# One decoder layer in a software pipeline on one core: the written-out order of four engines is replaced by another

## The chip, the cores and the metric

The kernel runs on 1 core of one Trainium2 chip. The time is device microseconds (us) of that core, from the start to the end of one launch. Five engines work side by side, each taking its own instructions strictly in program order: TensorE (PE in the profile; its weight loads stand apart as PEld), VectorE (DVE), ScalarE (ACT), GpSimd (POOL) and SyncE (SP, which here only starts DMAs). They wait for one another on semaphores alone.

## The reference

The input x is 64 sequences of 128 rows of 512 numbers, in f32. Three blocks, each with a residual and a layer norm in front of it:

```python
x = x + _L0_attn_ref(_layernorm(x), ...)            # state-space mixer
x = x + _L0_xattn_ref(_layernorm(x), ctx, ..., 64)  # banded attention, gated by ctx
x = x + _L0_ffn_ref(_layernorm(x), ...)             # 8 experts, the best 2 used
```

The mixer, with I = 1024 channels, N = 16 states per channel and R = 128:

```python
proj = x @ in_proj_w.T ; h_in, gate = split(proj)
u  = silu(causal_conv4(h_in) + conv_b)
ts, Bm, Cm = split(u @ x_proj_w.T)
dt = softplus(ts @ dt_proj_w.T + dt_proj_b)
dA = exp(dt[..., None] * -exp(A_log)) ; dBx = (dt * u)[..., None] * Bm
h  = scan(h * dA + dBx)                   # along the 128 rows
y  = ((h * Cm).sum(states) + D * u) * silu(gate)
out = y @ out_proj_w.T
```

The attention has 8 heads of 16 over a band of 64 to either side, then relu, a product with ctx and one more matrix. The last block is a softmax router over 8 experts with 16 hidden channels each.

## The kernel before

**Groups.** The 64 sequences are taken two at a time: 32 groups (`NG`). Within one iteration of every engine's program up to four groups are in work: the scans of group g (`cur`), the projections and step sizes of group g+1 (`nxt`), the attention of group g-1 (`p1`) and the experts of group g-2 (`p2`). Iterations -1, 0, 1 and the last four are written out, the others stand in a hardware loop of two iterations each.

**The core of it: 64 scan steps per group.** Step s is one block of 128 channels (`ic = s // 8`) and one pair of states (`r = s % 8`), 512 numbers per partition. For each step
- ACT writes the decays into one of two PSUM slots (`decays`, two `Exp` of L474, the slot is `s % DAR`). It may do so when scan s-2 is done; where the state of s-2 was kept in PSUM (`s % 8` in 1, 4, 7), when DVE's product with C is done too (L470 then clears the first column);
- POOL writes dt·u·B into one of eight ring slots in SBUF (`times_b`, L306), once PE has added up step s-8 (`hc_used`);
- DVE runs the scan (`scan`, L1498);
- the product with C is POOL's (`times_c`, L315, 40 steps) or DVE's (`times_c`, L1482, 24 steps, those with `s % 8` in 1, 4, 7);
- PE adds the products of two steps at a time by transposing matmuls into PSUM (`y_sum`, L1114).

**The other work** stands between these steps: `h_in`, `gate_in`, `ts_in`, `dt_in`, `out_proj` and the parts of the attention (`proj`, `v`, `s`, `shift`, `st`, `av`, `den`, `rep`, `wo`, `ct`) on PE; conv (L1601), the maxima of the scores (`max`, L1520), `addq`, `on`, `enc`, `x2`, the router and `y_step` (L1491) on DVE; the exps of the attention (L628), silu (L580 of u, L593 of the gate, L645 of the experts), copies out of PSUM and norms on ACT.

**The step size.** softplus is taken apart: ACT makes |z|, exp, +1 and ln (`soft_exp`, `soft_one`, `soft_ln`), DVE four steps per pair of channel blocks (`soft_step` 1 to 4: L1466, L1469, L1473, L1477), 128x512 each. These sixteen DVE instructions per group read two tensors that both lie in SBUF; the scans, L1482 and the conv read one of their operands from PSUM. `soft_step(4)` makes du, for which `times_b` waits at every 16th step.

**ScalarE's tables.** Exp, Silu and Ln need a table each; the compiler puts an ACT_TABLE_LOAD ahead of the first function of another kind. A stretch of another table between two `decays` is called an excursion here: one load to get there, one to come back.

**What sets the order.** Nothing at run time: `iteration(g, cur, nxt, p1, p2)` of each engine is a list of calls written out by hand, with the work of the four groups interleaved. SP's list is not touched.

Of the kernel before, what the change touches and what calls it, by code (L numbers as in the profile page):

```python
# [5 lines left out]
def decoder_layer(nc, x_d, ctx_d, w_in_d, conv_w_d, conv_b_d, w_xt_d, w_xbc_d, w_dt_d, dt_b_d, a_log_d,  # L6
# [40 lines left out]
    with stack:  # L47
# [233 lines left out]
        def _(pool):  # L281
# [37 lines left out]
            def iteration(g, cur, nxt, p1, p2):  # L319
                if p1:  # L320
                    times_c(g - 1, 62)
# [3 lines left out]
                if p2:  # L325
                    rstd("e", g - 2, 0, 2)
                if cur:
                    times_b(g, 2)
                    times_b(g, 3)
                    times_c(g, 0)  # L330
# [6 lines left out]
                    times_b(g, 8)  # L337
                    times_b(g, 9)
                    times_b(g, 10)
                    times_c(g, 5)  # L340
                if p1:
                    rstd("t", g - 1, 0)
                if cur:
                    times_b(g, 11)
                    times_b(g, 12)
                    times_b(g, 13)
                    times_c(g, 6)
                    times_c(g, 8)
                    times_c(g, 10)
                    times_b(g, 14)  # L350
                    times_c(g, 11)
                    times_b(g, 15)
                if nxt:
                    rstd("a", g + 1, 0, 2)
                if cur:
                    times_b(g, 16)
                    times_b(g, 17)
                    times_c(g, 13)
                    times_b(g, 18)
                    times_c(g, 14)  # L360
                    times_b(g, 19)
                    times_b(g, 20)
                    times_c(g, 16)
                    times_c(g, 18)
                    times_b(g, 21)
                    times_b(g, 22)
                    times_b(g, 23)
                    times_b(g, 24)
                    times_c(g, 19)
# [3 lines left out]
                    times_b(g, 26)  # L373
                if p1:
                    rstd("t", g - 1, 1)
                if cur:
                    times_b(g, 27)
# [3 lines left out]
                    times_b(g, 30)  # L381
                    times_c(g, 26)
                    times_c(g, 27)
                    times_b(g, 31)
                    times_c(g, 29)
                    times_b(g, 32)
                    times_c(g, 30)
                    times_b(g, 33)
                    times_b(g, 34)
                    times_b(g, 35)  # L390
                    times_c(g, 32)
                    times_b(g, 36)
                    times_b(g, 37)
                    times_b(g, 38)
                    times_c(g, 34)
                    times_b(g, 39)
# [7 lines left out]
                    times_b(g, 44)  # L404
# [1509 lines left out]
```

How the kernel before makes its waits and increments, by code:

```python
        def reached(engine, semaphore, count):  # L194
            if not (isinstance(count, int) and count <= 0):
                engine.wait_ge(semaphore, count)
# [25 lines left out]
            def iteration(g, cur, nxt, p1, p2):  # L223
# [5 lines left out]
                    piece(1, 0)  # L229
                if p1:
                    context((g - 1) * GB)
                if cur:
                    for r in range(NSPREAD, RS):
                        spread(g, r)
                if nxt:
                    reached(sp, gin_ps, j * NQ)
                    piece(0, 1)
                if p2:
                    sp.wait_ge(x3_done, (g - 1) * GB)
                    sp.dma_start(rows(out_d, g - 2), x_att[:]).then_inc(x_out, 16)
                if nxt:
                    sp.wait_ge(hin_ps, j * NQ + 1)
                    piece(1, 2)
                    sp.wait_ge(hin_ps, j * NQ + 2)
                    piece(0, 3)
                    sp.wait_ge(gin_ps, j * NQ + 1)
                    piece(1, 4)
                    sp.wait_ge(hin_ps, j * NQ + 3)
                    piece(0, 5)
                if p1:
                    context((g - 1) * GB + 1)
                if nxt:
                    sp.wait_ge(gin_ps, j * NQ + 2)
                    piece(1, 6)
                    sp.wait_ge(hin_ps, j * NQ + 4)
                    piece(0, 7)
                    sp.wait_ge(bc_made, j + 1)
                    for c in range(4):
                        sp.dma_start(bc_d.rearrange("r (k t) -> (r k) t", k=4)[:, c * (NT // 4):(c + 1) * (NT // 4)],
```

## Time and profile before

| | us |
|---|---|
| median of 3 runs (lowest, highest) | 5135.03 (5134.79, 5142.79) |
| the profiled execution, its own time | 5140.37 |
| its span in the profile | 5138.5 |
| granted TensorE clock over the span | 0.975 of full speed |
| busy: PE / DVE / POOL / ACT | 4659.6 / 4631.4 / 4395.1 / 4216.9 |

Four engines are busy for 82% to 91% of the span, so no one of them is plainly the bound. The start (until the first scan at 104 us) and the end (after the last one, near 4983 us) are thinly filled; between them the same pattern repeats, once per group. A period of the pattern is best read off a DMA that SP starts once per group, the store of the result.

### The profile page before, as it was taken

To read this page: it belongs to the slowest core of one execution; us is meant where nothing else is said; L and a number is where in the kernel's file an instruction comes from. 1 tells how busy PE (TensorE), PEld (TensorE's weight loads), DVE (VectorE), ACT (ScalarE), POOL (GpSimd) and SP (SyncE) were. 2 spreads that over 40 slices of the span, in tenths; PEclk is the share of its full clock that TensorE was granted. 3 is DMA by queue.
4 is the path that set the end of the run, shared out by engine and by line. 5 is a ranking of instruction groups with operands and counts; after the bars stand their busy time and mean duration, and the time that the engine had idled before them with its cause. 6 is when DMAs were issued, how large, how long until landed. Compare 5 with 4: busy or idle time off the path is not lost.

```text
span 5138.5 us, 143326 instructions
## 1 busy us (share of the span) xinstructions
PE 4659.6 (91%) x52548; PEld 3356.2 (65%) x52548; DVE 4631.4 (90%) x6051; ACT 4216.9 (82%) x8962; POOL 4395.1 (86%) x3467
## 2 busy tenths in 40 slices
PE   4799999999999999999999999999999999999986
PEld 3566666666666766666666666666666666666653
DVE  3899999999999999999999999999999999999962
ACT  3788888888888888888888888888888888888862
POOL 2988998988898988999988998898889898889870
PEclk8899999999999999999999999999999999999986
DMA  3212222212222211222221222221222221222200
GB/s 120 77 41 71 69 76 79 80 47 69 74 75 76 80 62 54 75 73 76 79 80 37 79 69 80 79 80 40 77 69 75 80 80 49 67 73 72 67 10 11
DMA packets 119316, 350.46 MB, mean 68 GB/s; under 512 B 18688, under 2 KB 19456, under 8 KB 118528
## 3 DMA queue, kind: packets, MB, share of 16 engines
q1 hardware_dynamic: 118656, 341.51, 20.2%
q8 instruction: 432, 7.08, 0.6%
q14 instruction: 228, 1.87, 0.1%
HBM read 323.64 MB, written 17.83 MB: 66 GB/s over the span
## 4 chain that ended last, share of the span: by engine, by line
PE 44%; issue 16%; POOL 16%; DVE 12%; ACT 11%; POOLq 0%; DVEq 0%; ACTq 0%; DMA 0%
POOL ring L306 10%; PE ps L1162 8%; PE ps L1114 6%; POOL ring L315 5%; PE ps L1182 5%; PE ps L1058 4%; PE ps L1069 3%; PE ps L1030 3%; DVE nmax L1520 3%; DVE ring L1498 3%; ACT ps L474 2%; PE ps L1005 2%; ACT probs_mem L628 2%; DVE hc L1601 2%; PE ps L1094 2%
## 5 line engine op out<-in xcount | busy, mean ns | idle before, releaser
L306 POOL TENSOR_TENSOR ring<-du,bc 128x512 f32<-128x512 f32 x2048 | 2640.6, 1309 | 374.6 <-PE ps L1114 276.8
L315 POOL TENSOR_TENSOR ring<-ring,bc 128x512 f32<-128x512 f32 x1280 | 1715.4, 1350 | 185.6 <-DVE ring L1498 180.2
L474 ACT ACTIVATE ps<-delta,a_neg 128x254 f32<-128x254 f32 x4096 | 1767.6, 469 | 114.7 <-DVE ring L1498 103.5
L1498 DVE TENSOR_TENSOR_SCAN ring<-ps,ring 128x512 f32<-128x512 f32 x1280 | 1536.2, 1211 | 45.6 <-ACT ps L474 30.8
L1114 PE MATMUL ps<-ident,ring 128*128 128x128 f32 x8192 | 1090.0, 279 | 45.1 <-POOL ring L315 39.7
L1114 PEld LDWEIGHTS ps<-ident,ring 128*128 128x128 f32 x8192 | 932.4, 143 | 243.8 <-issue 172.3
L1498 DVE TENSOR_TENSOR_SCAN ps<-ps,ring 128x512 f32<-128x512 f32 x768 | 935.2, 1218 | 123.6 <-ACT ps L474 119.0
L1482 DVE TENSOR_TENSOR ring<-ps,bc 128x512 f32<-128x512 f32 x768 | 526.4, 685 | 12.4
L1182 PE MATMUL ps<-w_in,xt_a 128*128 128x256 f32 x2048 | 484.6, 391 | 37.7 <-ACT yz L562 20.1
L628 ACT ACTIVATE probs_mem<-ps 128x768 f32<-128x768 f32 (+1 forms) x512 | 441.8, 908 | 52.6 <-PE ps L1058 50.1
L1162 PE MATMUL ps<-xt_a,w_in 128*128 128x256 f32 x2048 | 476.8, 386 | 7.4 <-DVE hc L1601 4.1
L1144 PE MATMUL ps<-w_outp,yz 128*128 128x512 f32 x1024 | 467.1, 599 | 6.7 <-DVE x_att L1544 6.7
L1182 PEld LDWEIGHTS ps<-w_in,xt_a 128*128 128x128 f32 x2048 | 387.0, 194 | 114.2 <-issue 43.9
L1520 DVE TENSOR_REDUCE nmax<-ps 128x8 f32<-128x1280 f32 x256 | 379.8, 1484 | 68.5 <-PE ps L1030 61.8
L1162 PEld LDWEIGHTS ps<-xt_a,w_in 128*128 128x128 f32 x2048 | 382.1, 191 | 80.8 <-issue 25.4
L1601 DVE SCALAR_TENSOR_TENSOR hc<-ps,conv_w,hc 128x254 f32<-128x254 f32 (+2 forms) x768 | 360.5, 473 | 63.2 <-ACT hc L573 42.2
L470 ACT COPY ps<-zeros 128x4 f32<-128x4 f32 x768 | 126.9, 165 | 251.0 <-DVE ring L1482 244.4
L1144 PEld LDWEIGHTS ps<-w_outp,yz 128*128 128x128 f32 x1024 | 189.2, 192 | 205.6 <-issue 193.9
L1030 PE MATMUL ps<-qk 32*32 32x160 f32 (+2 forms) x16384 | 294.6, 296 | 0.0
L1058 PE MATMUL ps<-qk 32*128 32x192 f32 (+1 forms) x4096 | 274.4, 383 | 0.0
L1005 PE MATMUL ps<-xb,w_qk 128*128 128x512 f32 x512 | 252.8, 607 | 15.4 <-ACT qk L615 12.6
L1069 PE MATMUL ps<-probs_mem,v_aug 128*32 128x192 f32 (+1 forms) x4096 | 229.0, 366 | 10.2 <-ACT probs_mem L628 10.2
(139 smaller groups left out, 6550.3 us busy)
## 6 DMA issues: line engine op xcount, KB each, us to landing
w_in<-in_w_in SPq DMA_DIRECT2D x256, 512.0 KB, 3.6
bc<-bc_rows SPq DMA_DIRECT2D x256, 512.0 KB, 5.9
x_new<-in_x SPq DMA_DIRECT2D x32, 512.0 KB, 6.1
x_res<-in_x SPq DMA_DIRECT2D x32, 512.0 KB, 5.0
enc<-in_ctx SPq DMA_DIRECT2D x64, 256.0 KB, 3.8
out<-x_att SPq DMA_DIRECT2D x32, 512.0 KB, 3.0
w_outp<-in_w_outp SPq DMA_DIRECT2D x1, 2048.0 KB, 8.2
bc_rows<-bc_sb SPq DMA_DIRECT2D x128, 8.0 KB, 1.4
```

What stands on the lines that cost most here:

```text
L306: nc.gpsimd.tensor_tensor(ring[:, s % RING, :].rearrange("p (n t) -> p n t", n=2), du[:, q % 2, (ic % 2) * NT:(ic % 2 + 1) * NT].rearrange ...
L315: nc.gpsimd.tensor_tensor(ring[:, s % RING, :], ring[:, s % RING, :], bc[:, s % RS, 2:4, :].rearrange("p a t -> p (a t)"), ALU.mult).then_ ...
L474: nc.scalar.activation(ps[:, s % DAR, (n % 2) * NT:(n % 2 + 1) * NT].rearrange("p (b t) -> p b t", b=GB)[:, :, 1:T], delta[:, ic, :].rearr ...
L628: nc.scalar.activation(probs[:, :, blk, lo:hi], ps[:, PS_ATT:PS_ATT + 4, (n % 2) * WIN + lo:(n % 2) * WIN + hi], ACT.Exp).then_inc(p_done, 1)
L1058: last = nc.tensor.matmul(ps[:, PS_ATT + hp, a * WIN + lo:a * WIN + hi], qk[r:r + 32, 2 + j, blk * P:(blk + 1) * P], qk[r:r + 32, j, at:at ...
L1114: last = nc.tensor.matmul(ps[:, PS_Y, b * T:(b + 1) * T], ring[:, t % RING, n * NT + b * T:n * NT + (b + 1) * T], ident[:], start=False, s ...
L1144: last = nc.tensor.matmul(ps[:, PS_ATT + b, :], yz[:, ic, b * T:(b + 1) * T], w_outp[:, ic, :], start=(ic == 0), stop=(ic == NI - 1))
L1162: last = nc.tensor.matmul(ps[:, PS_B, a * NT:(a + 1) * NT], w_in[:, slot, k, a * P:(a + 1) * P], xt_a[:, k, :], start=(k == 0), stop=(k == ...
L1182: last = nc.tensor.matmul(ps[:, PS_B, b * NT:(b + 1) * NT], xt_a[:, k, b * T:(b + 1) * T], w_in[:, slot, k, :], start=(k == 0), stop=(k == ...
L1482: nc.vector.tensor_tensor(ring[:, s % RING, :], ps[:, s % DAR, :], bc[:, s % RS, 2:4, :].rearrange("p a t -> p (a t)"), ALU.mult).then_inc ...
L1498: nc.vector.tensor_tensor_scan(state, ps[:, s % DAR, :], ring[:, s % RING, :], 0.0, ALU.mult, ALU.add).then_inc(h_done, 1)
L1520: nc.vector.tensor_reduce(nmax[:, n].rearrange("p j (a r) -> p a j r", r=32)[:, :, :, DH], ps[:, PS_ATT:PS_ATT + 4, 0:NJ * NEAR].rearrange ...
```

## The change

In `iteration` of POOL, ACT, PE and DVE the calls stand in another order. Every call is there as often as before, with the same arguments, so the same buffers and the same semaphores; SP's list and all helper functions are as they were. ScalarE's helper functions stand one line higher up than before, PE's four lines further down, DVE's where they were. As the order decides where ScalarE changes its table, the number of table loads is not the same: 60 in the program before, 72 now, which is 10 and 12 in one iteration with all four groups.

The diff is 1185 lines of moved calls; its shape, in DVE's list:

```diff
                 if cur:
                     scan(g, 4)
                     times_c(g, 4)
+                    soft_step(1, g, 2)
+                    scan(g, 5)
                     soft_step(4, g, 1)
-                    scan(g, 5)
                     scan(g, 6)
+                    soft_step(2, g, 2)
                     scan(g, 7)
...
                 if cur:
-                    scan(g, 60)
+                    times_c(g, 60)
+                if p1:
+                    attention(g, 1, "x2")
                 if nxt:
                     soft_step(1, j, 0)
```

and in PE's, second sequence of the attention:

```diff
                 if p1:
                     attention(g, p2, 1, "s", 3)
-                if cur:
-                    y_sum(g, 35)
-                    y_sum(g, 37)
+                if nxt:
+                    h_in(j, 3, cur)
                 if p1:
                     attention(g, p2, 1, "shift")
```

**VectorE, the end of iteration 1.** `L1498` is a scan, `L1482` DVE's product with C, `L1538` is `enc`, `L1544` is `x2` of the second sequence, `L1466`, `L1469`, `L1473` and `L1477` are `soft_step` 1 to 4 of group g+1. Before:

```order
L1538 SCALAR_TENSOR_TENSOR o_sb<-ps,enc 128x512
L1498 SCALAR_TENSOR_TENSOR ps<-ps,ring 128x512
L1466 SCALAR_TENSOR_TENSOR tmp<-tmp,soft 128x512
L1482 TENSOR_TENSOR ring<-ps,bc 128x512
L1466 SCALAR_TENSOR_TENSOR tmp<-tmp,soft 128x512
L1498 SCALAR_TENSOR_TENSOR ring<-ps,ring 128x512
L1469 SCALAR_TENSOR_TENSOR delta<-delta,tmp 128x512
L1498 SCALAR_TENSOR_TENSOR ring<-ps,ring 128x512
L1473 TENSOR_TENSOR delta<-delta,soft 128x512
L1544 SCALAR_TENSOR_TENSOR x_att,ln_sum_e<-ps,b_ct,x_res 128x512
L1477 TENSOR_TENSOR du<-delta,u 128x512
L1498 SCALAR_TENSOR_TENSOR ps<-ps,ring 128x512
```

The same place now, to the end of the iteration:

```order
L1538 SCALAR_TENSOR_TENSOR o_sb<-ps,enc 128x512
L1482 TENSOR_TENSOR ring<-ps,bc 128x512
L1544 SCALAR_TENSOR_TENSOR x_att,ln_sum_e<-ps,b_ct,x_res 128x512
L1466 SCALAR_TENSOR_TENSOR tmp<-tmp,soft 128x512 x2
L1469 SCALAR_TENSOR_TENSOR delta<-delta,tmp 128x512
L1498 SCALAR_TENSOR_TENSOR ring<-ps,ring 128x512
L1469 SCALAR_TENSOR_TENSOR delta<-delta,tmp 128x512
L1498 SCALAR_TENSOR_TENSOR ps<-ps,ring 128x512
L1473 TENSOR_TENSOR delta<-delta,soft 128x512
L1477 TENSOR_TENSOR du<-delta,u 128x512
L1482 TENSOR_TENSOR ring<-ps,bc 128x512
L1473 TENSOR_TENSOR delta<-delta,soft 128x512
```

The soft steps stood one by one between scans; three now follow each other ahead of scan 62, and two with the last product and one more behind scan 63, while `x2` comes two instructions after `enc`.

**ScalarE, the last silu of u in iteration 1.** `L573` is conv's first tap, `L580` silu of u, `L593` silu of the gate, `L562` and `L632` are copies out of PSUM, `L474` decays, `L628` exps of the attention. Before:

```order
L573 ACTIVATE hc<-ps,conv_b,conv_w 128x256 x2
L632 COPY o_sb<-ps 128x512
L580 ACT_TABLE_LOAD
L580 ACTIVATE u<-hc 128x512
L593 ACTIVATE gate_t<-gate_t 128x2x512
L580 ACTIVATE u<-hc 128x512
L562 COPY yz<-ps 128x256
L470 COPY ps<-zeros 128x4
L474 ACT_TABLE_LOAD
L474 ACTIVATE ps<-delta,a_neg 128x2x127 x4
```

Now (the same functions are one line number lower):

```order
L473 ACTIVATE ps<-delta,a_neg 128x2x127 x2
L627 ACTIVATE probs_mem<-ps 128x4x256
L627 ACTIVATE probs_mem<-ps 128x4x192
L473 ACTIVATE ps<-delta,a_neg 128x2x127 x2
L579 ACT_TABLE_LOAD
L579 ACTIVATE u<-hc 128x512
L561 COPY yz<-ps 128x256
L631 COPY o_sb<-ps 128x512
L469 COPY ps<-zeros 128x4
L473 ACT_TABLE_LOAD
L473 ACTIVATE ps<-delta,a_neg 128x2x127 x4
```

One excursion with three silus has become a short one with one silu, two decays later; the silu of the gate has an excursion of its own five decays earlier, and the third silu went to the others of u.

## Rows read from the trace of the kernel before

**Rows 1.** The page: its head, and each engine's busy us (share) xinstructions.
```profile
span 5138.5 us, 143326 instructions
PE 4659.6 (91%) x52548; PEld 3356.2 (65%) x52548; DVE 4631.4 (90%) x6051; ACT 4216.9 (82%) x8962; POOL 4395.1 (86%) x3467
```

**Rows 2.** Busy time by stretch: PE, PEld, DVE, ACT, POOL, clock, DMA share, GB/s.
```profile
2420.40:3031.40 611.00, 572.38 (x6568) 413.55 (x6568) 578.51 (x757) 526.35 (x1120) 549.76 (x433) 1.00 0.22 71
```

**Rows 3.** Timeline of SP: start, duration, issue of the result's store, four groups apart.
```profile
2420.42 0.40 SPq L240 DMA_DIRECT2D out<-x_att  x1
...
3031.38 0.40 SPq L240 DMA_DIRECT2D out<-x_att  x1
```

**Rows 4.** Groups of DVE, 2420.4 to 3031.4: busy us, mean ns, idle before.
```profile
L1498 DVE TENSOR_TENSOR_SCAN ring<-ps,ring 128x512 f32<-128x512 f32 x160 | 192.1, 1211 | 3.1 <-ACT ps L474 2.0 <-POOL ring L306 0.9
...
L1482 DVE TENSOR_TENSOR ring<-ps,bc 128x512 f32<-128x512 f32 x97 | 66.5, 685 | 1.5
...
L1601 DVE SCALAR_TENSOR_TENSOR hc<-ps,conv_w,hc 128x254 f32<-128x254 f32 (+2 forms) x96 | 45.1, 473 | 2.6
L1466 DVE SCALAR_TENSOR_TENSOR tmp<-tmp,soft 128x512 f32<-128x512 f32 x16 | 19.4, 1212 | 0.0
L1469 DVE SCALAR_TENSOR_TENSOR delta<-delta,tmp 128x512 f32<-128x512 f32 x16 | 17.5, 1091 | 0.0
L1473 DVE TENSOR_TENSOR delta<-delta,soft 128x512 f32<-128x512 f32 x16 | 17.2, 1074 | 0.0
L1477 DVE TENSOR_TENSOR du<-delta,u 128x512 f32<-128x512 f32 x16 | 13.5, 842 | 0.0
L1491 DVE TENSOR_TENSOR yg<-ps,gate_t 128x256 f32<-128x256 f32 x32 | 13.1, 408 | 0.0
```

**Rows 5.** One line's instructions, same stretch: duration ns min/median/max.
```profile
L1473 DVE TENSOR_TENSOR delta<-delta,soft x16: 659/914/1815, 2438.7 to 2996.1; 128x512 f32<-128x512 f32 x16
```

**Rows 6.** Timeline, one soft step of DVE and POOL's neighbours.
```profile
2531.40 1.28 POOL L306 TENSOR_TENSOR ring<-du,bc 128x512 f32<-128x512 f32 x1
2531.41 1.81 DVE L1473 TENSOR_TENSOR delta<-delta,soft 128x512 f32<-128x512 f32 x1
...
2532.62 1.73 POOL L315 TENSOR_TENSOR ring<-ring,bc 128x512 f32<-128x512 f32 x1
```

**Rows 7.** Timeline, the end of ScalarE's longest excursion; brackets: idle before, releaser.
```profile
2504.20 1.28 ACT L474 ACT_TABLE_LOAD   x1
...
2505.49 1.66 ACT L474 ACTIVATE ps<-delta,a_neg 128x254 f32<-128x254 f32 x4
2506.39 1.23 DVE L1498 TENSOR_TENSOR_SCAN ps<-ps,ring 128x512 f32<-128x512 f32 x1 [2.93 <-ACT ps L474]
```

**Rows 8.** Groups of ACT, 2420.4 to 3031.4.
```profile
L562 ACT COPY yz<-ps 128x256 f32<-128x256 f32 x32 | 11.8, 369 | 15.6 <-PE ps L1135 15.6
...
L580 ACT ACTIVATE u<-hc 128x512 f32<-128x512 f32 x16 | 10.0, 626 | 0.1
...
L632 ACT COPY o_sb<-ps 128x512 f32<-128x512 f32 x16 | 9.3, 583 | 4.4 <-PE ps L1069 4.4
```

**Rows 9.** Timeline of DVE: two waits for PE, at `max` and at `experts_add`.
```profile
2479.76 1.49 DVE L1520 TENSOR_REDUCE nmax<-ps 128x8 f32<-128x1280 f32 x1 [1.16 <-PE ps L1030]
...
2572.65 0.69 DVE L1508 TENSOR_TENSOR x_att<-ps,x_att 128x512 f32<-128x512 f32 x1 [1.35 <-PE ps L1235]
```

**Rows 10.** Timeline of PE: one `h_in`, and its wait for the router.
```profile
2469.65 3.72 PE L1182 MATMUL ps<-w_in,xt_a 128*128 128x256 f32 x16
...
2568.55 0.65 PE L960 MATMUL ps<-ident,probs_mem 128*128 128x128 f32 x2 [1.55 <-DVE probs_mem L1590]
```

**Rows 11.** Timeline of the start: POOL's first product with B, the first scan.
```profile
98.09 5.77 POOL L306 TENSOR_TENSOR ring<-du,bc 128x512 f32<-128x512 f32 x4 [74.23 <-DVE du L1477]
...
104.17 1.22 DVE L1498 TENSOR_TENSOR_SCAN ring<-ps,ring 128x512 f32<-128x512 f32 x1 [3.88 <-ACT ps L474]
```

More of the change, by code:

```diff
@@ L827, in iteration @@
                 if cur:
-                    decays(g, 42)
-                if p1:
-                    attention(g, p2, 1, "exp", 0)
-                    attention(g, p2, 1, "exp", 1)
-                if cur:
-                    decays(g, 43)
                     decays(g, 44)
@@ L838, in iteration @@
                     decays(g, 45)
+                if nxt:
+                    gate_silu(j, 0)
+                if cur:
+                    decays(g, 46)
+                    decays(g, 47)
+                if nxt:
+                    tap3(j, 3)
+                if cur:
+                    skip_term(g, 7)
+                if p1:
+                    attention(g, p2, 1, "exp", 0)
+                    attention(g, p2, 1, "exp", 1)
+                if cur:
+                    decays(g, 48)
+                    decays(g, 49)
                 if p1:
@@ L856, in iteration @@
                     y_back(g, 4)
-                    decays(g, 49)
-                    decays(g, 50)
+                if p1:
+                    attention(g, p2, 1, "o", 0)
+                if cur:
+                    decays(g, 51)
+                    decays(g, 52)
                 if p1:
@@ L1265, in iteration @@
                     attention(g, p2, 0, "proj", 0)
+                    attention(g, p2, 0, "proj", 1)
+                if cur:
+                    y_sum(g, 5)
+                if p2:
+                    experts_gate(g - 2)
+                if p1:
+                    attention(g, p2, 0, "v")
+                if p2:
+                    experts_up(g - 2)
                 if cur:
@@ L1346, in iteration @@
                 if p1:
-                    attention(g, p2, 1, "s", 1)
+                    attention(g, p2, 0, "wo")
+                    attention(g, p2, 1, "proj", 1)
+                if cur:
+                    y_sum(g, 31)
                 if nxt:
@@ L1370, in iteration @@
                 if cur:
[L1371 to L1373 removed]
+                    y_sum(g, 47)
+                    y_turn(g, 4, nxt)
                 if p1:
@@ L1675, in iteration @@
                     scan(g, 18)
-                if p1:
-                    attention(g, 0, "max", 2)
-                if cur:
-                    scan(g, 19)
                     y_step(g, 1)
@@ L1697, in iteration @@
                 if cur:
+                    scan(g, 23)
+                if nxt:
+                    conv(j, 1)
+                if cur:
+                    times_c(g, 23)
                     scan(g, 24)
@@ L1734, in iteration @@
                 if cur:
-                    scan(g, 34)
+                    scan(g, 37)
+                    y_step(g, 3)
+                    scan(g, 38)
+                    scan(g, 39)
                 if p1:
@@ L1779, in iteration @@
                     conv(j, 6)
+                if cur:
+                    scan(g, 48)
+                if nxt:
                     conv(j, 7)
                 if cur:
-                    scan(g, 48)
+                    y_step(g, 5)
                     scan(g, 49)
@@ L1793, in iteration @@
                     times_c(g, 55)
+                    scan(g, 56)
+                    scan(g, 57)
+                    y_step(g, 6)
+                    times_c(g, 57)
                 if p1:
@@ L1802, in iteration @@
                 if cur:
-                    y_step(g, 6)
-                    scan(g, 58)
-                    scan(g, 59)
+                    scan(g, 60)
+                    scan(g, 61)
                 if p1:
```

551 lines of the change are left out of this document (255 added, 296 removed).

## The prediction, made before the changed kernel ran

> **What bounds the kernel now.** The page's first part comes first: PE, DVE and POOL are busy for 86% to 91% of the span [rows 1]. That is a mean over a thin start, 32 groups and a thin end, so the next view is the timeline of SP: the store of the result is issued at 2420.42 and, four groups later, at 3031.38 [rows 3]. A group takes 610.96 / 4 = 152.74 us. The busy time over the same stretch [rows 2] divided by four gives, per group, PE 143.1, DVE 144.6, POOL 137.4, ACT 131.6; idle are PE 9.6, DVE 8.1, POOL 15.3, ACT 21.2. So DVE has the least air, PE nearly as little, and a new order can gain in two ways alone: fewer of DVE's 8.1 idle microseconds, or DVE instructions that themselves take less. 32 groups have 31 distances between them; with 31 I multiply.
>
> The second way exists. DVE's groups [rows 4] show the scan at 1211 ns, and the four soft steps, which read two operands from SBUF, at 1212, 1091, 1074 and 842 ns. The shortest of L1473 took 659 ns, the longest 1815 [rows 5]. The timeline shows why [rows 6]: this longest one is entered at 2531.41, just after a POOL product that started at 2531.40 and took its usual 1.28; it ends at 2533.22, that is 0.54 us after the POOL product, and the next POOL product, entered at 2532.62, takes 1.73 in place of 1.28. The two take turns. The scans show nothing of it, they are as long beside POOL as without.
>
> **The change, part by part, in us per group.**
>
> (a) *Soft steps.* The mean of the four is (1212 + 1091 + 1074 + 842) / 4 = 1055 ns; alone it would be 659. Each pays 0.40, all sixteen 6.3. To be rid of it a soft step has to stand where POOL waits. Now three of group g+1 follow one another between `x2` and scan 62. POOL has at most one product with C (of step 61) and one with B (63) left then, since the next, step 62's, waits for scan 62. The first soft step meets a product, the second and third should not. Behind scan 63 POOL's next product with B is step 0 of the next group and waits for du, so `soft_step` 3 and 4 ahead of that should be free too. One more, `soft_step(4, g, 3)`, follows `addq` of the second sequence, where POOL waits for the `y_sum` behind PE's long block. Five of sixteen, 5 x 0.40 = -2.0. The bounds are 0 (POOL late at all of them) and -6.3 (all sixteen free). I take -2.0, since the other eleven stand between scans as before.
>
> (b) *ScalarE's longest excursion.* At scan 49 DVE waits 2.93 for decays that come behind two silus of u, one of the gate and a reload [rows 7]. Now the silu of the gate has an excursion of its own, with a scan, a maximum and a product of DVE beside it, and the last silu of u stands between decays 50 and 51. From the end of scan 48, ACT does decays 50 (a pair, 1.66 / 2 = 0.83 [rows 7]), load 1.28, silu 0.63, two copies 0.37 and 0.58 [rows 8], load 1.28, decays 51 0.83: 5.8. DVE has in the meantime three conv taps (3 x 0.47), `y_step` 0.41, two scans of 1.21, one product 0.69 [rows 4]: 4.9 by durations, some 4.5 as they overlap at their ends. It waits about 1.4. Gain 2.93 - 1.4: -1.5. Bounds: -2.9 and 0.
>
> (c) *Table loads.* Two more per group, 2 x 1.28 = 2.6 on ACT [rows 7]. The decays are issued at most two scans ahead, so an excursion costs when DVE has less than its length to do; the three new borders lie beside conv, maxima and `addq`. Cost 0, covered by ACT's 21.2 idle; 2.6 if that cover were gone. In the timeline the first exp follows the load's start by 1.29 us (2504.20 to 2505.49 [rows 7]), so 1.28 is the whole price. The Trainium skill, "ScalarE: Activation LUTs", section "What ACT_TABLE_LOAD costs", says about 1283 ns of load plus 1380 ns of drain, 2.66 us for every switch; the load agrees to the nanosecond, the drain is not there in this trace. By the page the excursion of (b) would last 2.8 longer and eat its gain of 1.5, and the sum below would come out near +0.8 in place of -2.0; the trace decides.
>
> (d) *DVE's waits for PE that go.* 1.16 at the third `max` of the second sequence and 1.35 at `experts_add` [rows 9]. The first came from an `h_in` that PE did ahead of those scores; now they follow the `max` before with two sums between, while DVE has two scans and a product. The second came from a `y_sum` ahead of `experts_up`, which now stands behind it. -2.5, bounds 0 and -2.5.
>
> (e) *New short waits.* Five places where DVE now asks sooner for what another engine has just been told to do: `router(1)` directly behind `router(0)` (an exp of ACT lies between); `x2` two instructions after `enc` (PE's `ct` lies between); `soft_step(3)` of g+1, whose `soft_ln` moved behind a gate copy to the very end of ACT's list; `addq` of both sequences, as `h_in` was put ahead of `shift` on PE. The trace has no such waits; the nearest rows are 1.16 and 1.35 [rows 9], the largest 2.93 [rows 7], the least is 0. I take 0.8 each, below the nearest rows since part is covered by the instructions between: +4.0; bounds 0 and 5 x 2.93 = 14.7.
>
> (f) *PE and POOL.* PE gets 9.6 idle and its list has the same work. In its early part `out_proj` of the second sequence and the norm's transposes went ahead of `y_sum(1)`, so the sums of steps 1 to 7 come about 5 us later, and POOL waits for these before step 9 to 15. Their cover is that DVE has the router before scan 11 now. PE's own wait for the router, 1.55, stays. Cost 0; if the cover is gone, up to one `h_in`, 3.72 [rows 10].
>
> Sum: -2.0 - 1.5 - 2.5 + 4.0 = -2.0 per group, 31 x -2.0 = -62.
>
> (g) *Start and end.* POOL begins at 98.09, the first scan at 104.17 waits 3.88 for ACT [rows 11]. Now du comes about 2 us later (ACT does the third step size and the gate copy before `soft_ln`), but the decays follow it after one step size instead of a copy, a skip term and a step size. First scan some 2 us earlier: -2. The end has the same chain of attention and experts: 0, within 5 either way.
>
> The profiled execution's own time is 5140.4, 5.3 above the median. 5140.4 - 64 = 5076; against the median of 5135.0 that is 5071. I say 5073.
>
> **The rivals.**
>
> *R1, slower: a whole `h_in` between `s` and `shift`.* In both sequences PE has `h_in` (3.72 [rows 10]) between the last scores and the transposes for which `addq` waits. DVE used to have one scan (first sequence) or one conv (second) between its fourth `max` and `addq`, now two scans and one scan. If DVE is as early as before, it waits 3.72 less one scan of 1.21 in the first and all 3.7 in the second, 6.2 together. With the other three waits of (e) at 0.8 that makes -2.0 - 1.5 - 2.5 + 2.4 + 6.2 = +2.6 per group, +81, less 2: 5219 of its own, 5214 against the median. It decides from 3.6 on (the two waits together), where the sum is 0. For it: DVE is the fullest engine and cannot catch up. Against it: PE lags DVE by several scans, `h_in` could start while the fourth `max` runs, and the wait that leads to the sum is also taken off elsewhere (`st` no longer has `h_in` behind it).
>
> *R2, even: given back.* The waits of (e) come to 1.2 each (the nearest rows' size): 6.0, the sum is 0.0. Or POOL is late and (a) gives nothing. 5135. For it: in the stretch all four engines are busy for 86% or more [rows 2], so what one gains another soon asks for.
>
> *R3, the waits of (e) are all covered.* -2.0 - 1.5 - 2.5 = -6.0, x 31 = -186, less 2: 4952 of its own, 4947. For it: DVE would be idle 2 us of some 147, which no stretch of this trace comes near to. Half way, 5010, is more likely.
>
> *R4, the ports are not what the order serves.* POOL gets late by other waits and the soft steps stay at 1055 ns; (b) and (d) still hold: the sum is 0, as R2, which includes it.
>
> **How the numbers follow.** Forecast 0.45, with a range of its own from 5020 to 5120. R3 and half of it 0.14 (4947 to 5020). R2 with R4 0.14 (5120 to 5150). R1 0.27 (5146 to 5215 and above). What a measurement of this kernel can tell from no change is 0.2%, 10 us. Faster: 0.45 + 0.14 + 0.03 of R2 = 0.62; same: 0.09; slower: 0.27 + 0.02 = 0.29. The range leaves out some 0.07 below and 0.12 above: 4985 to 5190.
>
> **What would show it.** The store of the result every 150.7 us in place of 152.7. (a) L1466 to L1477 at a mean near 930 ns in place of 1055, and of the six soft steps of g+1 up to du, four near 0.66. (b) No DVE wait for ACT of over 2 us; one near 1.4 at scan 51. (c) 12 table loads per group, the exp right behind each. (d) the third `max` and `experts_add` without a wait. (e) waits of 0.5 to 1.4 at `addq`, `x2`, `soft_step(3)` and the router; R1 is right if the two `addq` wait 3.6 or more together, R3 if none waits. (f) POOL's waits for `y_sum` in the early part stay under 2. The forecast is wrong in its base if DVE's idle time per group grows above 11 us.

## The result, and the profile after

| | before | after |
|---|---|---|
| median (lowest, highest) of 4 runs each | 5136.00 (5134.79, 5142.79) | 5098.34 (5097.39, 5103.19) |
| the profiled execution, its own time | 5140.37 | 5097.39 |
| ratio, 95% interval | | 0.9926, [0.9909, 0.9943] |

The changed kernel is 38 us faster, against 62 forecast. The page's head after, to be held against [rows 1]:

```profile
span 5095.5 us, 143390 instructions
PE 4632.5 (91%) x52548; PEld 3377.4 (66%) x52548; DVE 4539.5 (89%) x6051; ACT 4303.2 (84%) x9026; POOL 4273.2 (84%) x3467
```

DVE has the same 6051 instructions and is busy 92 us less; ACT has 64 instructions more, the table loads. A stretch of four groups, from store to store (timeline of SP) and its busy times, answers to [rows 2, 3]:

```profile
2402.13 0.40 SPq L240 DMA_DIRECT2D out<-x_att  x1
...
3009.50 0.40 SPq L240 DMA_DIRECT2D out<-x_att  x1
```

```profile
2402.10:3009.50 607.40, 570.70 (x6568) 417.01 (x6568) 565.89 (x757) 537.04 (x1129) 534.12 (x433) 0.99 0.22 71
```

A group takes 607.37 / 4 = 151.84 in place of 152.74. DVE is busy 141.5 of it (before 144.6) and idle 10.4 (before 8.1): its instructions became 3.1 shorter, and 2.3 of that went into waits. Only 0.9 of the 3.1 is in the soft steps (67.6 us before and 63.8 now in four groups). Most of the rest is in three small instructions of the router, of which the prediction had nothing: before, they ended with a product of POOL (L1574 of 2564.85 ended at 2565.73, 0.03 behind one), and now POOL mostly waits beside them. They took 10.6 us in four groups and take 3.6, 1.8 less per group. Two of them, before:

```profile
L1581 DVE COPY small<-small 128x4 f32<-128x4 f32 x4 | 3.4, 851 | 0.1
L1574 DVE TENSOR_TENSOR small<-small 128x16 f32<-128x16 f32 x4 | 3.0, 756 | 0.6 <-DVE small L1572 0.6
```

and after:

```profile
L1581 DVE COPY small<-small 128x4 f32<-128x4 f32 x4 | 0.7, 170 | 0.1
L1574 DVE TENSOR_TENSOR small<-small 128x16 f32<-128x16 f32 x4 | 0.9, 232 | 0.1
```

The third is L1590, from 558 to 287 ns, eight times. The groups of DVE in this stretch, to be held against [rows 4]:

```profile
L1498 DVE TENSOR_TENSOR_SCAN ring<-ps,ring 128x512 f32<-128x512 f32 x160 | 192.3, 1210 | 16.8 <-ACT ps L473 15.8
...
L1473 DVE TENSOR_TENSOR delta<-delta,soft 128x512 f32<-128x512 f32 x16 | 30.0, 1877 | 4.5 <-ACT soft L547 4.5
...
L1469 DVE SCALAR_TENSOR_TENSOR delta<-delta,tmp 128x512 f32<-128x512 f32 x16 | 11.7, 734 | 0.0
L1466 DVE SCALAR_TENSOR_TENSOR tmp<-tmp,soft 128x512 f32<-128x512 f32 x16 | 11.3, 725 | 0.0
L1477 DVE TENSOR_TENSOR du<-delta,u 128x512 f32<-128x512 f32 x16 | 10.8, 674 | 0.1
```

Three of the four soft steps now take little more than the 0.66 us of one that meets no product of POOL (725, 734 and 674 ns). The fourth kind, L1473, went from 1074 to 1877. The view of that one line says that it is not all of them:

```profile
L1473 DVE TENSOR_TENSOR delta<-delta,soft x16: 672/1119/4600, 2433.3 to 2978.5; 128x512 f32<-128x512 f32 x16
```

One of the four per group takes 4.6 us. It is `soft_step(3, g, 2)`, behind scan 27. The timeline around it, DVE and POOL:

```profile
2432.38 1.28 POOL L306 TENSOR_TENSOR ring<-du,bc 128x512 f32<-128x512 f32 x1
2433.31 4.59 DVE L1473 TENSOR_TENSOR delta<-delta,soft 128x512 f32<-128x512 f32 x1
2433.61 2.51 POOL L315 TENSOR_TENSOR ring<-ring,bc 128x512 f32<-128x512 f32 x2
...
2436.07 1.28 POOL L306 TENSOR_TENSOR ring<-du,bc 128x512 f32<-128x512 f32 x1
...
2437.82 1.22 DVE L1498 TENSOR_TENSOR_SCAN ps<-ps,ring 128x512 f32<-128x512 f32 x1
...
2440.83 1.26 POOL L315 TENSOR_TENSOR ring<-ring,bc 128x512 f32<-128x512 f32 x1 [3.48 <-DVE ring L1498]
```

The step is entered while a product runs, POOL starts three more back to back, none of them longer than alone (2.51 for two), and the step ends at 2437.90, 0.55 behind the end of POOL's last at 2437.35. It had no turn in between. Then POOL waits 3.48 for the scans behind the step: POOL had held up the engine that it needed. I call such a step *starved*. It happens in every one of the 28 groups between 463 and 4558 us.

**Where the 43 us of the two profiled executions went.** The stores of all groups give a second surprise: the distances are not equal. Busy time by stretch of two neighbouring groups, before:

```profile
1349.87:1502.12 152.25, 142.73 (x1642) 102.96 (x1642) 144.25 (x190) 131.51 (x280) 137.28 (x109) 1.00 0.22 71
1502.12:1656.09 153.97, 144.21 (x1646) 104.48 (x1646) 145.01 (x190) 131.64 (x280) 138.14 (x109) 0.99 0.21 70
1648.00:1650.00 2.00, 0.68 (x7) 0.49 (x5) 1.93 (x8) 1.97 (x5) 1.84 (x2) 1.00 0.00 0
1650.00:1652.00 2.00, 1.76 (x9) 1.76 (x10) 2.00 (x4) 1.87 (x3) 0.70 (x1) 0.61 0.00 0
1652.00:1654.00 2.00, 2.00 (x7) 1.39 (x6) 0.99 (x3) 1.55 (x3) 1.85 (x2) 0.53 0.01 4
```

The lower three are slices of the second: PE is idle for most of 1648 to 1650 (its 1.55 us wait for the router [rows 10]), and right behind it the granted clock is near half, the lower level of 1.2 GHz, for some 3.4 us. Such a stretch is called a fall here. Eleven groups of the kernel before have one, ten of them behind that wait, and are some 1.4 us or more too long. After:

```profile
1491.91:1643.53 151.62, 142.76 (x1646) 105.50 (x1646) 141.48 (x191) 134.41 (x284) 133.59 (x109) 0.99 0.21 71
1643.53:1796.41 152.88, 143.60 (x1642) 104.31 (x1642) 141.30 (x189) 134.06 (x282) 133.45 (x109) 0.99 0.21 71
```

Falls are as many (13), but ten of them come some 40 us into the group, behind a wait of 2.21 that PE now has for the products held up by the starved step. There DVE is late anyway, and eight of these groups, the first row is one, are only 0.1 longer than their neighbours. Three come some 87 us in, behind a wait of 1.66 at `y_turn` (PE's transposes of what `y_step` made). Two of them cost 1.6 each (the second row is one); the third is in a group that has both kinds of fall and is 2.8 too long.

So: between the stores at 432.71 and 4871.29 before (432.20 and 4830.67 after) lie 29 groups. Undisturbed ones alternate between 152.25 and 152.46 before, 151.25 and 151.52 after; that is 0.97 each, 28 us. The surplus over that is 20.4 before and 8.4 after, 12 us. The start gives 0.5, the end 2.4. Sum 43.

Not all of the 12 is the clock's. Falls cost some 14.8 before and 7.0 after: 8 us. One soft step of 2.95 in the kernel before, at 1839, makes 1.2. Another 3 are in the group between the stores at 4560.56 and 4717.67, in which the first iteration behind the hardware loop begins: before, it is 4.7 too long, since ScalarE and PE stand there though nothing in the profile holds them ("issue"), and the fall comes only behind that; after (4526.41 to 4679.33) it is 1.4 too long. Before:

```profile
4683.65 1.06 ACT L534 ACTIVATE soft<-delta 128x1024 f32<-128x1024 f32 x1 [5.08 <-issue]
4685.46 2.50 PE L1182 MATMUL ps<-w_in,xt_a 128*128 128x256 f32 x5 [4.37 <-issue]
```

What makes these two waits, and why they are short after the change, no run shows.

### The profile page after: what moved, and what is told of

The parts are those of the page before. It is cut to its first block, busy times and chain, and to the rows that moved or that the text cites. A ratio compares the mean times of both kernels' runs of the same rounds, so it can differ in the third digit from the quotient of the medians.

```text
span 5095.5 us, 143390 instructions
## 1 busy us (share of the span) xinstructions
PE 4632.5 (91%) x52548; PEld 3377.4 (66%) x52548; DVE 4539.5 (89%) x6051; ACT 4303.2 (84%) x9026; POOL 4273.2 (84%) x3467
## 4 chain that ended last, share of the span: by engine, by line
PE 34%; POOL 24%; issue 19%; DVE 12%; ACT 8%; DMA 3%; DVEq 0%; POOLq 0%; ACTq 0%
POOL ring L306 13%; POOL ring L315 10%; PE ps L1118 6%; PE ps L1166 4%; DVE ring L1498 4%; PE ps L1186 3%; PE ps L1034 3%; DMA bc<-bc_rows 3%; PE ps L1073 2%; PE ps L1195 2%; DVE hc L1601 2%; ACT ps L473 2%; DVE ps L1498 2%; PE ps L1009 2%; PE ps L1098 2%
## 5 line engine op out<-in xcount | busy, mean ns | idle before, releaser
L306 POOL TENSOR_TENSOR ring<-du,bc 128x512 f32<-128x512 f32 x2048 | 2600.7, 1292 | 371.0 <-DVE du L1477 204.4
L315 POOL TENSOR_TENSOR ring<-ring,bc 128x512 f32<-128x512 f32 x1280 | 1668.6, 1314 | 180.5 <-DVE ring L1498 180.5
L1498 DVE TENSOR_TENSOR_SCAN ring<-ps,ring 128x512 f32<-128x512 f32 x1280 | 1538.3, 1210 | 141.4 <-ACT ps L473 129.3
L1118 PE MATMUL ps<-ident,ring 128*128 128x128 f32 x8192 | 1069.1, 278 | 133.8 <-POOL ring L315 130.6
L1498 DVE TENSOR_TENSOR_SCAN ps<-ps,ring 128x512 f32<-128x512 f32 x768 | 931.7, 1213 | 12.4 <-ACT ps L473 5.0
L1482 DVE TENSOR_TENSOR ring<-ps,bc 128x512 f32<-128x512 f32 x768 | 522.3, 680 | 7.0
L1473 DVE TENSOR_TENSOR delta<-delta,soft 128x512 f32<-128x512 f32 x128 | 239.7, 1872 | 35.7 <-ACT soft L547 35.7
```

The costliest lines, as they stand in the source:

```text
L306: nc.gpsimd.tensor_tensor(ring[:, s % RING, :].rearrange("p (n t) -> p n t", n=2), du[:, q % 2, (ic % 2) * NT:(ic % 2 + 1) * NT].rearrange ...
L315: nc.gpsimd.tensor_tensor(ring[:, s % RING, :], ring[:, s % RING, :], bc[:, s % RS, 2:4, :].rearrange("p a t -> p (a t)"), ALU.mult).then_ ...
L1118: last = nc.tensor.matmul(ps[:, PS_Y, b * T:(b + 1) * T], ring[:, t % RING, n * NT + b * T:n * NT + (b + 1) * T], ident[:], start=False, s ...
L1482: nc.vector.tensor_tensor(ring[:, s % RING, :], ps[:, s % DAR, :], bc[:, s % RS, 2:4, :].rearrange("p a t -> p (a t)"), ALU.mult).then_inc ...
L1498: nc.vector.tensor_tensor_scan(state, ps[:, s % DAR, :], ring[:, s % RING, :], 0.0, ALU.mult, ALU.add).then_inc(h_done, 1)
```

## The experiments

Ratios are to the kernel before, run on the same chip each time.

**e1: the starved step two scans earlier.** VectorE's list of the changed kernel:

```diff
                     scan(g, 25)
+                    soft_step(3, g, 2)
...
                     scan(g, 27)
-                    soft_step(3, g, 2)
```

> The changed kernel with one VectorE instruction moved: soft_step(3, g, 2) stands behind scan 25 in place of behind scan 27. In the changed kernel it takes 4.59 us in every group, as POOL has three products in a row beside it. Theory A (it is starved at SBUF by POOL, and the scan and PE's sums behind it pay): it takes 0.7 to 1.8 us here, POOL's wait of 3.48 for scan 29 and PE's of 2.21 for POOL's product shrink to under 1 each, the clock no longer falls behind PE's gap there, and the store comes every 149.5 to 150.5 us in place of 151.4: 5040 to 5070. Rival B (the 4.59 are slack, another chain sets the period): the step is short, the idle time turns up elsewhere on DVE, and the time stays at 5098 within 8. Rival C (the length is not from POOL): it takes 4 us again in its new place.

5038.15 us, ratio 0.9801 [0.9786, 0.9816]; the interval lies clear of the changed kernel's. The step in its new place takes 0.67:

```profile
2399.07 0.56 POOL L294 TENSOR_TENSOR ln_rs_t<-ln_rs_t,neg_half 128x1 f32<-128x1 f32 x1
2399.36 0.67 DVE L1473 TENSOR_TENSOR delta<-delta,soft 128x512 f32<-128x512 f32 x1
2399.59 1.57 POOL L306 TENSOR_TENSOR ring<-du,bc 128x512 f32<-128x512 f32 x1
```

The undisturbed groups take 148.5 and 148.8, 2.7 less. PE's wait of 2.21 and the falls behind it are gone; five falls some 84 us in, behind the wait of 1.66 at `y_turn`, stay. Theory A, a little beyond its numbers (5040 to 5070, a store every 149.5 to 150.5). One instruction's place was worth 60 us, more than the whole rewriting had brought.

**e2 and e6: the soft steps back at their old places.** In e2 all of them, in e6 only the nine of group g, as `soft_step(2, g, 2)` and `(3, g, 2)` behind scans 21 and 22.

> The changed kernel with all soft steps of VectorE put back to where the kernel before has them in relation to the scans; nothing else is touched. Theory A (the prediction's term a: the new places are worth what their durations show, 67.6 us in four groups before against 63.8 after, 0.95 per group): 5098 + 31 x 0.95 = 5127, with the steps again near 1.05 us on the mean. Rival B (the starved step costs as much as the others gain): the mean goes up but the 4.59 us step is gone too, the time stays at 5098 within 10 or falls below.

> The changed kernel with the nine soft steps of groups g at the places of the kernel before in relation to the scans; the seven of group g+1 at the end of the list stay as changed (they had taken part in e2 and brought waits of their own for ACT). Theory A (one step starved costs the 4.59 us that it takes; the others take turns): one of the nine is longer than 3 us and the time is near 5098, or none is and it is near 5038 plus 31 x 0.4 to 1.2, 5050 to 5075. Rival B (the old places cost by themselves): above 5110 though no step is longer than 2 us.

e2: 5374.29, ratio 1.0465 [1.0450, 1.0479], 160.4 per group. Both theories fell; part of it is the experiment's own doing: with soft_step 1 behind scan 60 DVE waits 3.15 for ACT, and POOL 4.32 for du. In e2, too, a step is starved, 3.7 us in every group. e6 leaves the end of the list out: 5195.26, ratio 1.0094 [1.0079, 1.0109], 154.2 to 155.7 per group, and another step than in the changed kernel is starved in every group, `soft_step(2, g, 2)`, for 3.67:

```profile
L1469 DVE SCALAR_TENSOR_TENSOR delta<-delta,tmp 128x512 f32<-128x512 f32 x12 | 18.4, 1531 | 0.0
L1466 DVE SCALAR_TENSOR_TENSOR tmp<-tmp,soft 128x512 f32<-128x512 f32 x12 | 13.7, 1160 | 0.0
```

(three groups). All sixteen steps take 18.2 per group, in e1 13.0. Both theories of e6 fell as well: A had the time near 5098 with one starved step, B had no step over 2 us. The shorter groups take 154.3, against 151.4 in the changed kernel and 148.6 in e1: the new places in the middle are worth 2.9 us per group with everything else of the change in place, and 5.7 with the starved step moved. The clock is not taken out of this: PE waits 3.06 once per group in e6, and each of these waits has a fall. So with the new order of the other engines the old places in the middle are three times as bad as the whole change is good (1.0 per group); in the kernel before the same places starve a step in one group of 29.

**e7: the places at the end of the list alone, in the kernel before.** The two `soft_step` 1 and the first 2 stand ahead of scan 62, `soft_step(2, j, 1)` behind x2, and:

```diff
                     scan(g, 63)
+                if nxt:
+                    soft_step(3, j, 0)
+                    soft_step(4, j, 0)
```

> The kernel before with the soft steps of group g+1 alone placed as in the changed one: two soft_step 1 and one soft_step 2 ahead of scan 62, soft_step 2 of the second pair behind x2, soft_step 3 and 4 behind scan 63. In the kernel before these seven take 7.8 us together. Theory A (term a of the prediction): five of the seven near 0.66, together 5.5, and the store 1 to 2 us sooner: 5075 to 5105. Rival B (du comes later, POOL's first product of the next group waits for it, 0.8 now, 2.8 in the changed kernel): the steps get shorter as in A, and the time stays at 5135 within 10. Rival C: a step of them is starved for over 3 us, 5150 and more.

5236.30, ratio 1.0164 [1.0148, 1.0181], 155.7 per group. Of the seven steps only three are near 0.66; two meet a product from its start and take 1.76 and 1.77, and together the seven take 8.4 in place of 7.8. POOL's first product of the next group waits 3.25 for du, 0.80 before:

```profile
2747.09 2.96 POOL L306 TENSOR_TENSOR ring<-du,bc 128x512 f32<-128x512 f32 x2 [3.25 <-DVE du L1477]
```

This is rival B's wait, at a price (3.4 per group) that B did not have; the time is in rival C's range, but no step is starved. The places on which term (a) mostly rested are a loss by themselves: they are free only where POOL's list is the new one.

**e5 and e9: the port by itself.** Neither computes the layer; both copy x and send VectorE's step into a row of POOL's products at an entry that shifts by 0.03 and 0.01 us.

```python
for k in range(4):      # POOL, e5
    nc.gpsimd.tensor_tensor(ring[:, k, :], du[:], bc[:], ALU.mult)
...                     # VectorE
nc.vector.tensor_copy(flat[:, 2048:2048 + cols], flat[:, 0:cols])
nc.vector.tensor_tensor(tmp[:], delta[:], soft[:], ALU.add)
```

> Not the layer: a kernel that measures the port alone and otherwise only copies x. 180 times POOL multiplies two SBUF tensors into a ring slot four times in a row (128x512, as times_b), started together with VectorE, which does a copy inside PSUM of 16 + 30 n columns (n = 0 to 59) and right behind it one instruction on 128x512: 60 times an add of two SBUF tensors (as soft_step 3), 60 times a scalar_tensor_tensor of two SBUF tensors (as soft_step 1), 60 times an add of a PSUM and an SBUF operand. Theory A (turns, as the prediction has it): the first two kinds take at most the rest of POOL's product plus 0.55, so 0.66 to 1.85, whatever the entry; the third is always 0.68. Theory B (a band of entries starves): for entries in one part of POOL's product, from about 0.6 us behind its start on, the instruction gets no turn at all and lasts until POOL's fourth product is over, up to 4 us or more, and for entries in the other part it takes its turn. Theory C (it hangs on what POOL waits for in the layer, not on the entry): no starving here at all.

> Again the port alone, now with the layer's own instructions: POOL runs a times_c, a times_b, two times_c and a times_b in a row (128x512 each, the same layouts, each waiting on a semaphore that is already met), VectorE a copy inside PSUM of 16 + 11 n columns (n = 0 to 119), two scans (in the second 120 trials one scan) and then soft_step 3 in place. e5 had no starving in any of its 120 entries. Theory C1 (what VectorE did before, or the mixture of POOL's products, makes the starving): in a part of the entries the step lasts until POOL's fifth product is over, 2 to 5 us, as the 4.59 in the changed kernel. Theory C2 (it hangs on a meeting with something else in the layer, finer than these instructions): the step takes its turn in all 240 entries, 0.66 to 1.8.

The three kinds of e5 (add, scalar_tensor_tensor, add with a PSUM operand), then e9's step:

```profile
L63 DVE TENSOR_TENSOR tmp<-delta,soft x60: 680/1259/1771, 6.5 to 335.1; 128x512 f32<-128x512 f32 x60
```

```profile
L65 DVE SCALAR_TENSOR_TENSOR tmp<-delta,soft x60: 680/1274/1771, 338.8 to 667.3; 128x512 f32<-128x512 f32 x60
```

```profile
L67 DVE TENSOR_TENSOR tmp<-ps,soft x60: 679/681/683, 671.0 to 973.0; 128x512 f32<-128x512 f32 x60
```

```profile
L83 DVE TENSOR_TENSOR delta<-delta,soft x240: 662/1182/1787, 14.5 to 1630.8; 128x512 f32<-128x512 f32 x120
```

In all 360 entries with two SBUF operands the step takes its turn: 0.66 to 1.79, at most the rest of POOL's product and 0.55, and POOL's next product is then 0.45 longer. With one operand in PSUM it is always 0.68. Theories A (and with it C) and C2: what makes a starved step is in neither kernel. It isn't the entry alone either, nor the kind of step: in the layer steps were starved that entered 0.6 (e6), 0.9 (the changed kernel) and 1.1 us (e3) behind the start of a product, and in e1, in the odd group at 4640, one that entered 0.06 behind; and in the changed kernel 30 steps that entered 0.8 to 0.9 us behind took their turn. This stays open.

**e4: PE's wait for the router filled, in the kernel before.**

```diff
-                if p2:
-                    experts_gate(g - 2)
                 if cur:
                     y_sum(g, 9)
                 if p2:
+                    experts_gate(g - 2)
                     experts_up(g - 2)
```

> The kernel before with one call of PE moved: y_sum(g, 9) ahead of experts_gate(g - 2) in place of behind it, so that PE's wait of 1.55 us for the router is filled with work that it has anyway. In the kernel before the granted clock falls to half for about 3.4 us right behind that wait in 11 of the groups, each of which is 1.4 to 1.7 us longer. Theory A (the fall follows PE's gap): no fall at that place, the long groups there are gone, -15 us; and the sum no longer stands between the router and experts_up, so DVE's wait of 1.35 at experts_add shrinks, up to -1.0 per group: 5135 - 15 - 0..31 = 5090 to 5120. Rival B (the clock falls in some groups whatever PE does there): falls as many and as costly as before, 5105 to 5135. Rival C: y_sum(9) itself waits for its products and the router's transposes come later: slower, above 5140.

5127.47, ratio 0.9985 [0.9976, 0.9994]. No fall is left between 400 and 4700 us. The eleven executions have a granted clock of 0.978 to 0.980 over the span, those of the kernel before beside them 0.975 to 0.980. DVE's wait at `experts_add` is gone too, and it brings nothing: undisturbed groups take 152.25 and 152.49, as before. So theory A is right on the falls and wrong on the second half, and the time lies outside its 5090 to 5120.

```profile
1350.80:1503.09 152.29, 142.84 (x1642) 102.81 (x1642) 144.27 (x190) 131.58 (x280) 137.44 (x108) 1.00 0.22 71
...
1044.11:1198.33 154.22, 143.02 (x1642) 102.84 (x1642) 146.19 (x190) 131.61 (x280) 136.49 (x108) 1.00 0.21 70
```

The second row is one of three groups that are 1.9 too long at full clock. Each of the three has a `soft_step` 1 of 3.4 us, at 538, 1150 and 3894, which takes 0.9 in the other groups; the kernel before has another such step, 2.95 at 1839. They give back some 5 of the 14 us that the falls had cost. Starving also strikes now and then where the order usually gets by.

**e12: the other wait of PE filled, on top of e1.**

```diff
-                    y_turn(g, 4, nxt)
                 if p1:
                     attention(g, p2, 1, "av", 0)
                 if cur:
+                    y_turn(g, 4, nxt)
```

> e1_step3_moved with one more call moved, on PE: y_turn(g, 4) behind av(g-1, 1, 0) in place of ahead of it. In e1 PE waits 1.66 us there for DVE's y_step, and right behind that wait the granted clock falls to half for some 3.3 us in five groups, each 1.6 us longer (150.1 to 150.4 in place of 148.5 to 148.8); the falls behind the 2.21 us gap of the changed kernel are gone in e1 together with that gap. Theory A (a fall follows a gap of PE of about that length and costs where PE is waited for): the gap is at most 1 us, the five falls are gone, -8 us; beyond that the groups are as long as in e1 (148.6), since PE's work is only swapped, up to 0.4 shorter: 5018 to 5032. Rival B (falls come in any case somewhere): as many falls elsewhere, 5038 within 8. Rival C: ScalarE's copy of y comes later and its decays with it, or a soft step is starved by the shift: above 5050.

5025.72, ratio 0.9785 [0.9772, 0.9799], the fastest median, in theory A's range. In the profiled execution (5018.74) PE waits 0.82 and 0.80 there, no fall is left between 410 and 4700 us, and every group up to 4452 takes 148.5 or 148.8:

```profile
2370.87:2519.65 148.78, 141.59 (x1646) 103.86 (x1646) 138.61 (x191) 134.33 (x284) 134.43 (x109) 1.00 0.22 73
2519.65:2668.18 148.53, 141.31 (x1642) 103.64 (x1642) 138.29 (x189) 133.97 (x282) 134.07 (x109) 1.00 0.22 73
```

In both, theory A says that a fall follows such a gap of PE and goes with it. e4 bears it out: ten of 29 groups had a fall behind that gap, and with the gap cut to 0.46 none has; the clocks of the eleven executions fit. e12 alone would not. The other four executions are 5 to 10 us longer than the profiled one, at a clock of 0.975 to 0.976 against its 0.978, and the intervals of e1 and e12 overlap. Nor does such a gap always bring falls: the same wait of 1.66 at `y_turn` stands in some 28 groups of each of four kernels, and has falls behind it in 5 of them in e1, 3 in the changed kernel, 1 in e10 and none in e8.

**e8: two table loads fewer**, on top of e1, in ScalarE's list:

```diff
+                    gate_silu(j, 0)
                     u_silu(j, 3)
```

(taken from its own excursion behind decays 45)

> e1_step3_moved with one call of ScalarE moved: the silu of gate(g+1, 0) ahead of the last silu of u, in the same excursion, so that one iteration has 10 table loads as in the kernel before and 2.6 us less of ScalarE's time. Theory A (term c of the prediction, the two loads are covered, and the long excursion costs DVE a wait): DVE's wait for the decays behind it, 1.75 in e1, grows to 2.8, and the time is 5038 to 5070. Rival B (ScalarE's time is on the path somewhere): 4980 to 5025, as 1 to 2 us per group come back.

5034.58, ratio 0.9781 [0.9763, 0.9799]. DVE's wait for the decays behind the excursion grows from 1.75 to 2.53, and the undisturbed groups take 148.9 and 149.15, 0.4 more than in e1. Nearer to theory A, though the time is between its range and B's: the two loads that the split costs are covered, and the split is worth having. The time is not longer than e1's since e1 has five falls (8 us) and two odd groups at its end (154.5 and 153.3), and e8's profile has neither, though PE waits the same 1.66 at `y_turn`.

**e10: soft_ln ahead of the gate copy**, on top of e8:

```diff
+                    soft_ln(j, 0)
                     gate_raw(j, 2)
-                    soft_ln(j, 0)
```

> e8_fewer_loads with soft_ln of group g+1 ahead of gate_raw(g+1, 2) at the very end of ScalarE's list, as in the kernel before. In e8 DVE waits 1.14 at soft_step 3 behind it, and POOL 2.8 for du behind that. Theory A (this wait, one of the five of term e, is paid in full, since POOL has nothing else to do): 0.6 to 0.95 less per group, both waits shorter by as much, 5034 - 31 x 0.6 to 0.95 = 5005 to 5015. Rival B (POOL catches up elsewhere, it has air of 14 us per group): within 8 of 5034.

5106.48, ratio 0.9940 [0.9926, 0.9953]; 151 to 153 per group: undisturbed ones are over 2 us longer than in e8, and those of 153 have a fall besides, behind the wait of PE shown below. Both theories fell. The waits shrank as A said (1.14 to 0.22, POOL's for du 2.83 to 1.90), but the copy behind it holds up PE, and that the next decays:

```profile
2672.58 1.13 PE L1217 MATMUL ps<-ts,w_dt 128*128 128x256 f32 x4 [1.78 <-ACT gate_t L586]
2673.80 0.84 ACT L525 ACTIVATE delta<-ps,dt_b 128x256 f32<-128x256 f32 x2 [1.28 <-PE ps L1217]
...
2676.86 1.22 DVE L1496 TENSOR_TENSOR_SCAN ring<-ps,ring 128x512 f32<-128x512 f32 x1 [1.10 <-ACT ps L473]
```

**e11: h_in behind shift**, on top of e8, in both sequences:

```diff
-                    h_in(j, 0, cur)
-                if p1:
                     attention(g, p2, 0, "shift")
+                if nxt:
+                    h_in(j, 0, cur)
```

> e8_fewer_loads with PE's h_in(g+1, 0) and h_in(g+1, 3) behind shift in place of ahead of it, as in the kernel before. Theory A (the rival R1 in its small form: only 0.6 of wait at addq hangs on it): the 0.61 at addq goes, and the time is within 10 of 5034. Theory B (R1 in full, PE's 3.7 us stand in DVE's way): 15 or more faster. Theory C (the h_in were put ahead for a reason: DVE's conv and POOL's next sums come later now): 15 or more slower.

5246.24, ratio 1.0207 [1.0193, 1.0221], 154 to 159 per group. Theory C, and by far: ACT stands before the conv's first tap and the decays behind it are late.

```profile
2649.34 1.02 ACT L572 ACTIVATE hc<-ps,conv_b,conv_w 128x256 f32<-128x256 f32 x2 [4.29 <-PE ps L1164]
```

**e3: POOL's old list** in the changed kernel.

> The changed kernel with POOL's order of the kernel before; the other three engines as changed. Theory A (POOL's own order is worth little, it has 17 us of air per group): 5098 within 10, the starved step as long as it was. Rival B (the new order of VectorE only pays with the new order of POOL, the starved step or POOL's waits change): 10 to 40 slower, and which soft steps are long changes.

5781.98, ratio 1.1267 [1.1246, 1.1287], 174 per group: rival B, and far beyond its numbers. POOL waits 7.1 and 8.4 for PE's sums, since `rstd("a")` and `rstd("t")` stand later in the old list than DVE's new one asks for them (DVE waits 9.2 at `shift` for the first); the same step as in the changed kernel is starved, for 5.66. The lists are one schedule and can't be mixed. Nothing about the port alone follows from this run.

## Why the prediction was right or wrong

The direction and the range held; the forecast was 25 us too fast. That it came as near as that is in part luck: an undisturbed group became 0.97 shorter where the sum said 2.0, which is 30 us over 31, and another 12 came from what the sum did not contain. By its steps, per group:

(a) *Soft steps, -2.0.* Mis-sized twice, in opposite directions. The five places that were counted on did come out as said (0.68 twice ahead of scan 62, 0.69 twice behind 63, 0.68 behind the second `addq`), and so did the first ahead of scan 62 (0.69), which should have met a product. But "the other eleven stand between scans as before" failed: those are shorter as well, and with the starved one moved the sixteen take 13.0 in place of 16.9, -3.9 (e1). And "the two take turns" failed: the rows shown were of steps that did take turns [rows 5, 6], and one step of 4.59 gave 3.0 of the 3.9 back. In time it cost 2.7 per group, 84 us over 31. e1 got 60 of them: its falls and its two odd groups near the end, which hold starved steps of their own, take 10 more than the falls of the changed kernel, and its start and end are 12 longer. This is the step on which the prediction missed. It also looked for shorter instructions in the soft steps alone; the router's, 1.8 per group, became shorter by twice as much as they did (0.9).

(b) *The long excursion, -1.5.* The wait fell from 2.93 to 1.75 (1.4 was forecast), but a new one of 1.14 came at scan 56, behind two exps of the attention. DVE's waits for decays are 3.9 per group before and after, so the term brought nothing by itself. Against one merged excursion the split is worth 0.4 (e8).

(c) *Two more loads, 0.* Right, as far as e8 shows, which takes out the two loads and the split together. The exp again follows its load at once:

```profile
2491.32 1.28 ACT L473 ACT_TABLE_LOAD   x1
2492.61 1.66 ACT L473 ACTIVATE ps<-delta,a_neg 128x254 f32<-128x254 f32 x4
```

(d) *Waits for PE that go, -2.5.* They went, but a wait of DVE that goes isn't time that comes back: for the one at experts_add e4 shows it, 0. The other was not tried by itself.

(e) *New waits, +4.0.* They came to 3.3: 0.62 at the second addq and at x2, 1.14 at soft_step 3, 0.89 in the router, none at the first addq. One of 0.96 behind the router (L1504, for ScalarE) was not foreseen. e10 and e11 say what two of them buy: the orders that avoid them are slower by 2 and by 5 to 10 us per group.

(f) The cost held; POOL's early wait for `y_sum` is 1.8. But "PE's own wait for the router, 1.55, stays" failed: PE does not wait there any more, and the falls behind that wait are gone with it. (g) The first scan came 0.6 earlier, not 2.

The forecast knew nothing of PE's clock falling behind PE's own waits; some 8 of the 43 us came from there, as most falls moved to a place where they cost 0.1. Some 3 more came from the first iteration behind the loop and 1 from the soft step that was starved at 1839 in the kernel before. Without these the change would have brought 31.

R1 fell: `addq` waits 0 and 0.62, as PE does `h_in` while the fourth maximum runs (in the second sequence from 1.0 us ahead of it to 1.3 behind it), and e11 shows the same `h_in` to be needed there. R2 fell too: 38 us are clear of no change. e1 goes about two thirds of the way to R3's size (148.6, R3 had 146.7), by other means. R4 fell: three of the four kinds of soft step are at 0.67 to 0.73.

## What to carry to other kernels

Read the minimum, median and maximum of every line of VectorE with two SBUF operands: one starved instruction hides in a mean, and moving it by two scans was worth more than the new order of four engines. Read the small instructions too: a copy of four columns was 0.85 us long. Take the distances between a repeated mark for all groups, not over a few: what comes only in some of them (a clock that falls behind an idle matmul engine, a starved step) shows nowhere else; and compare such things over several executions, since one profile can have none by chance. And price a shorter wait by what its engine is waited for next: the one wait of DVE that was taken away by itself (e4) brought nothing, and taking away two of those that came (e10, e11) cost 2 and 5 to 10 us.

## What the runs showed of the hardware

- Two SBUF operands on VectorE against POOL's products (128x512, 1.27 us): usually turns, the step lasts until the product ends and at most 0.55 more, POOL's next product takes 0.45 longer (360 entries). One operand in PSUM: 0.68 whatever POOL does (60 entries).
- In the layer the same step can get no turn over two to five products in a row, the one that runs at its entry counted, and last 3.0 to 5.7 us, always to 0.55 behind POOL's last. What decides it is open.
- Small instructions in SBUF pay as well: the router's copy of 128x4, with one operand, took 0.85 beside POOL's products and 0.17 in the changed kernel, where it stands clear of them.
- TensorE's granted clock falls from full (2.4 GHz) to near half (1.2) for about 3.4 us right behind gaps of PE of 1.55, 1.66 and 2.21 us, in some groups and not in others: behind the 1.66, in 5, 3, 1 and none of some 28 groups of four kernels. Behind e6's gap of 3.06 it falls in each of the 28 groups. With the gap of 1.55 cut to 0.46 (e4) no fall is left in 4300 us.
